# The second attention's step reordered, and its band's trip through memory in two halves

## The reference, cut to what matters

```python
q = _heads(x @ Wq)                      # x after a layernorm; 16 heads of 64
k = _heads(ctx_t @ Wk); v = _heads(ctx_t @ Wv)          # 77 text rows
sim = jnp.einsum('bihd,bjhd->bhij', q, k) * SCALE
dist = jnp.clip(jnp.arange(77)[None, :] - jnp.arange(nq)[:, None], -16, 16) + 16
sim = sim + jnp.einsum('bihd,ijd->bhij', q, rel_k[dist]) * SCALE
attn = jax.nn.softmax(sim, axis=-1)
out = jnp.einsum('bhij,bjhd->bihd', attn, v) + jnp.einsum('bhij,ijd->bihd', attn, rel_v[dist])
out = out + stream(Wk_ip, Wv_ip, ctx_i) * (jnp.tanh(alpha) + 1.0)
out = out + stream(Wk_ap, Wv_ap, ctx_a) * (jnp.tanh(beta) + 1.0)
return out.reshape(b, nq, 1024) @ Wo + bo               # added to x by the caller
```

## Time and profile before

| what | value |
|---|---|
| median of 3 runs | 1164.21 us (1162.24 to 1169.32) |
| profiled execution, its own time | 1165.82 us |
| its span | 1164.0 us |
| mean granted TensorE clock | 0.961 of full |
| PE, PEld, DVE, ACT, POOL busy | 1009.1, 792.3, 665.6, 406.5, 386.7 us |

### The profile page before, as it was taken

One profiled execution on the slowest core, in us unless ns is written; L12 is line 12 of the kernel. 1 busy time (PEld: TensorE's weight loads), 2 busy tenths in 40 slices (PEclk: granted clock), 3 DMA queues, 4 the chain that ended last, 5 costly groups with the idle time before them and its releaser, 6 DMA issues. The chain is left out here.

```text
span 1164.0 us, 23711 instructions
## 1 busy us (share of the span) xinstructions
PE 1009.1 (87%) x7428; PEld 792.3 (68%) x7429; DVE 665.6 (57%) x1607; ACT 406.5 (35%) x877; POOL 386.7 (33%) x481
## 2 busy tenths in 40 slices
PE   4888888845899999979997999999998985899996
PEld 4676666743466666647365888888887964888885
DVE  2788877764233333321105777677676572699994
ACT  2554444421222222213332445444453441222221
POOL 1243333431122222235001554644544432133332
PEclk9999999967999999989999999999999987899998
DMA  4444444334811111136673679888887752011110
GB/s 120 126 141 141 137 138 133 128 122 160 293 45 45 45 42 48 45 96 233 239 241 112 167 212 224 200 229 211 209 226 187 175 142 49 28 42 41 41 32 28
DMA packets 193657, 153.41 MB, mean 132 GB/s; under 512 B 130368, under 2 KB 176960, under 8 KB 193472
## 3 DMA queue, kind: packets, MB, share of 16 engines
q1 hardware_dynamic: 173568, 93.70, 30.6%
q10 hardware_dynamic: 16960, 50.58, 11.7%
q0 software_dynamic: 3072, 8.39, 2.3%
HBM read 84.80 MB, written 67.83 MB: 131 GB/s over the span
## 5 line engine op out<-in xcount | busy, mean ns | idle before, releaser
L1462 POOL TENSOR_TENSOR c_soft<-c_soft,c_share 128x616 f32<-128x616 f32 (+2 forms) x96 | 71.7, 774 | 136.5 <-DVE c_share L1890 134.6
L968 POOL TENSOR_TENSOR b_up<-b_up,b_gate 128x512 f32<-128x512 f32 x39 | 49.4, 1267 | 189.0 <-DVE b_up L1095 189.0
L2176 PE MATMUL d_CV<-d_hp,ffn_tap 128*128 128x128 f32 x768 | 95.3, 282 | 3.8 <-DVE d_hp L2253 3.4
L2176 PEld LDWEIGHTS d_CV<-d_hp,ffn_tap 128*128 128x128 f32 x768 | 90.9, 197 | 7.9 <-DVE d_hp L2253 5.1
L494 PE MATMUL a_M<-early 128*128 128x128 f32 x512 | 73.3, 289 | 9.3 <-ACT early L411 9.3
L1029 PE MATMUL b_G<-moe_w,b_rowsT 128*128 x156 | 76.0, 610 | 3.1 <-ACT b_rowsT L977 2.7
L1060 PEld LDWEIGHTS b_Y<-moe_w,b_hidT 128*128 128x128 f32 x312 | 59.3, 190 | 25.1 <-issue 19.2
L1060 PE MATMUL b_Y<-moe_w,b_hidT 128*128 x312 | 73.8, 380 | 0.8 <-ACT b_hidT L993 0.8
L494 PEld LDWEIGHTS a_M<-early 128*128 128x128 f32 x512 | 63.4, 196 | 16.0 <-ACT early L411 7.5
L1029 PE MATMUL b_U<-moe_w,b_rowsT 128*128 x156 | 73.4, 593 | 0.0
L1092 DVE TENSOR_TENSOR b_gate<-b_G,moe_b 128x512 f32<-128x512 f32 x39 | 27.0, 692 | 71.1 <-PE b_G L1029 70.3
(11 more groups left out here) (234 smaller groups left out, 2286.6 us busy)
## 6 DMA issues: line engine op xcount, KB each, us to landing
rel_windows<-c_relw ACTq DMA_DIRECT2D x32, 816.0 KB, 6.3
c_bias<-rel_windows SPq DMA_DIRECT2D x16, 616.0 KB, 4.9
prob_rows<-c_soft SPq DMA_DIRECT2D x16, 616.0 KB, 5.4
moe_w<-in_L_Wl SPq DMA_DIRECT2D x16, 512.0 KB, 3.8
values<-c_soft ACTq DMA_DIRECT2D x15, 512.0 KB, 3.4
b_rows<-expert_lists SPq DMA_DIRECT2D x39, 128.0 KB, 2.1
expert_out<-b_out SPq DMA_DIRECT2D x39, 128.0 KB, 1.7
c_v<-values SPq DMA_DIRECT2D x16, 308.0 KB
```

The lines of the kernel that those rows point to most:

```text
L968: nc.gpsimd.tensor_tensor(up[p][:, :], up[p][:, :], gate[p][:, :], ALU.mult).then_inc(g["hid"], 1)
L1462: ins = nc.gpsimd.tensor_tensor(soft[p][:, hs, a:z], soft[p][:, hs, a:z], share[:, s, hs].unsqueeze(2).to_broadcast([P, HS, z - a]), ALU.mult)
L2176: ins = nc.tensor.matmul(CV[:, m, :], tap[:, m, k, :], hp[p][:, m, k:k + P], start=(k == 0), stop=(k == 2))
```

## The change

- PE's step: `rows` of b+2 come right behind the first scores; `queries` are two calls of `query`; one ready piece (the first key tile in an odd step, the first half of the queries in an even one) stands between `weighted` 2 and 3 of b-1; `bands` and `output` of b-1 come last. ACT's order follows.
- DVE and POOL work on the rows of b+3 instead of b+2, DVE at its step's end, ahead of `output`; `ends` of b-1 moves behind the first `shares`. The rows of batch 2 are made in the setup.
- The residual plus bias is kept for all 16 batches (`x2b`, 16 KB a partition) and made by DVE in `rows`; POOL's `residual` is gone. For batches 0 to 2 the folded part of the bias is added in the setup by one DVE instruction of 768 columns.
- `prob_out` and `band_in` go by halves of 8 heads, each `prob_out` behind its own half's `normalise`. SP's order at the step's end is now: both `prob_out`, `rel_in` of b+2, both `band_in`, the store.
- The windows' zeros are written to memory once in the setup, by two DMAs out of a tile of 112 zeros; the window DMAs write rows of 92 numbers a head, no longer one run of 8 x 204.
- `far` has 61 columns a head, not 77 (`tails` and `ends`).
- In the setup DVE waits for the small weights before the first `rows`, and for the values' landing before the steps.

```diff
-        x2b = [sb(f"c_x2b{p}", [P, D]) for p in two]
+        x2b = sb("c_x2b", [P, NB, D])
...
-        relw = [sb(f"c_relw{h}", [P, HS, RELW]) for h in two]
+        relw = [sb(f"c_relw{h}", [P, HS, RELW - REL_LO - 1]) for h in two]
...
-            def prob_out(b, i, p):
-                apart(sp, g["soft"], 2 * b + 2)
-                since(sp, s_pin[p], 16 * i)
-                sp.dma_start(prob_d[p][:, :, MAXREL:MAXREL + TEXT], soft[p][:, :, 0:TEXT]).then_inc(s_pout[p], 16)
-
-            def band_in(b, i, p):
-                sp.wait_ge(s_pout[p], 16 * (i + 1))
-
-
-                sp.dma_start(band[p][:, :, 0:NSTEP - 1], sheared(prob_d[p], 1, 1, P, NSTEP - 1)).then_inc(s_pin[p], 16)
+            def prob_out(b, i, p, h):
+                hs = slice(h * HS, (h + 1) * HS)
+                apart(sp, g["soft"], 2 * b + h + 1)
+                since(sp, s_pin[p], 32 * i)
+                sp.dma_start(prob_d[p][:, hs, MAXREL:MAXREL + TEXT], soft[p][:, hs, 0:TEXT]).then_inc(s_pout[p][h], 16)
+
+            def band_in(b, i, p, h):
+                hs = slice(h * HS, (h + 1) * HS)
+                sp.wait_ge(s_pout[p][h], 16 * (i + 1))
+
+
+                sp.dma_start(band[p][:, hs, 0:NSTEP - 1], sheared(prob_d[p][:, hs, :], 1, 1, P, NSTEP - 1, HS)).then_inc(s_pin[p], 16)
...
-            sp.wait_ge(g["x2"], 1)
-            load(2, 0)
+            for p in two:
+                sp.wait_ge(g["x2"], p + 1)
+                load(2 + p, p)
+            sp.wait_ge(s_clear, 1)
+            for p in two:
+                sp.dma_start(rel_d[p][:, :, 0:REL_LO + 1], zeros[:, :].unsqueeze(1).to_broadcast([P, NH, REL_LO + 1])).then_inc(s_blank, 16)
...
+            sp.wait_ge(s_blank, 32)
...
+                    prob_out(b, i, p, h)
+                if there(b + 2):
+                    rel_in(b + 2, i + 1, p)
+                for h in two:
+                    band_in(b, i, p, h)
                 if not first:
                     store(b - 1, 1 - p)
-                band_in(b, i, p)
-                if there(b + 2):
-                    rel_in(b + 2, i + 1, p)
...
-                nc.gpsimd.tensor_tensor(far[:, :, :], soft[p][:, :, 0:TEXT],
-                                        cst("behind_band").unsqueeze(1).to_broadcast([P, NH, TEXT]), ALU.mult).then_inc(g["tails"], 1)
+                nc.gpsimd.tensor_tensor(far[:, :, :], soft[p][:, :, MAXREL:TEXT],
+                                        cst("behind_band")[:, MAXREL:TEXT].unsqueeze(1).to_broadcast([P, NH, TEXT - MAXREL]), ALU.mult).then_inc(g["tails"], 1)
...
-            residual(0, 0)
 
             def steps(b, i, p, first, last):
-                if there(b + 2):
-                    inverse_std(b + 2, p)
-                if there(b + 3):
-                    gather(b + 3, 1 - p)
+                if there(b + 4):
+                    gather(b + 4, p)
                 for h in range(2):
                     normalise(b, p, h)
+                if there(b + 3):
+                    inverse_std(b + 3, 1 - p)
                 tails(b, p)
-                if there(b + 1):
...
             def windows(b, i, p):
 
-                lo, hi = REL_LO + 1, REL_LO + NREL
+                hi, end = NSTEP, RELW - REL_LO - 1
                 for h in two:
                     n, k = turns.next()
                     act.wait_ge(g["filled"], n + 1)
                     since(act, s_relout[h], 16 * b)
                     r, w = T[k][:, 0:HS * NSTEP].rearrange("p (h r) -> p h r", h=HS), relw[h]
-                    nc.scalar.activation(w[:, :, lo:hi], r, ACT.Copy)
-                    nc.scalar.activation(w[:, :, hi:RELW], r[:, :, NSTEP - 1:NSTEP].to_broadcast([P, HS, RELW - hi]), ACT.Copy)\
+                    nc.scalar.activation(w[:, :, 0:hi], r, ACT.Copy)
+                    nc.scalar.activation(w[:, :, hi:end], r[:, :, NSTEP - 1:NSTEP].to_broadcast([P, HS, end - hi]), ACT.Copy)\
                         .then_inc(g["emptied"], 1)
                     act.wait_ge(g["emptied"], n + 1)
                     since(act, s_relin[p], 16 * i)
-                    act.dma_start(rel_d[p][:, h * HS:(h + 1) * HS, :], w[:, :, :]).then_inc(s_relout[h], 16)
+                    act.dma_start(rel_d[p][:, h * HS:(h + 1) * HS, REL_LO + 1:RELW], w[:, :, :]).then_inc(s_relout[h], 16)
 
             def exps(b, p, h):
...
-                    behind(b - 1)
-                if p == 1 and there(b + 2):
-                    projected(kT, PAIR_TILES[:2])
-                    exps(b, p, 0)
-                    projected(kT, PAIR_TILES[2:])
-                    exps(b, p, 1)
+                    for k in range(4):
+                        probs(k)
+                exps(b, p, 0)
+                if p == 1 and ahead:
+                    projected(kT, PAIR_TILES[:1])
+                if not first:
+                    attended(b - 1, 0)
+                if p == 1 and ahead:
+                    projected(kT, PAIR_TILES[1:2])
+                if p == 0 and ahead:
+                    query(p, 0)
+                exps(b, p, 1)
+                if p == 1 and ahead:
+                    projected(kT, PAIR_TILES[2:3])
+                if not first:
+                    attended(b - 1, 1)
+                if p == 1 and ahead:
+                    projected(kT, PAIR_TILES[3:])
+                    query(p, 0)
+                if ahead:
+                    query(p, 1)
+                    windows(b + 2, i + 1, p)
                 if not first:
                     bands()
-                if there(b + 2):
-                    rows()
-                if p == 0 or not there(b + 2):
-                    for h in two:
-                        exps(b, p, h)
-                if there(b + 2):
-                    queries(p)
-                    windows(b + 2, i + 1, p)
 
             by_batch(steps)(act)
...
+                between[0]()
                 pe.wait_ge(s_vin[p], 16 * NS * (i + 1))
-                for k in range(4):
-                    weighted(b, p, k, n[k])
-                    if k < 2:
-                        n.append(probabilities(b, p, k + 2))
+                weighted(b, p, 0, n[0])
+                n.append(probabilities(b, p, 2))
+                weighted(b, p, 1, n[1])
+                n.append(probabilities(b, p, 3))
+                weighted(b, p, 2, n[2])
+                between[1]()
+                weighted(b, p, 3, n[3])
+
+            def nothing():
+                pass
 
             def steps(b, i, p, first, last):
                 turns.begin(b, i, p)
+                ahead = there(b + 2)
                 scores(b, i, p, 0)
+                if ahead:
+                    n_rows = rows(b + 2, p)
+
+                def second_scores():
+                    scores(b, i, p, 1)
+
+                def ready_work():
+                    if p == 1 and ahead:
+                        context(i + 1)
+                        projected(wk[0], PAIR_TILES[:1])
+                    elif ahead:
+                        query(n_rows, 0)
+
+                if first:
+                    second_scores()
+                    ready_work()
+                else:
+                    attend(b - 1, i - 1 + p, 1 - p, [second_scores, ready_work])
+                if p == 1 and ahead:
+                    projected(wk[0], PAIR_TILES[1:])
+                    query(n_rows, 0)
+                if ahead:
+                    query(n_rows, 1)
+                    distances(p)
                 if not first:
-                    n_probs = [probabilities(b - 1, 1 - p, 0), probabilities(b - 1, 1 - p, 1)]
-                scores(b, i, p, 1)
-                if not first:
-                    attend(b - 1, i - 1 + p, 1 - p, n_probs)
-                if p == 1 and there(b + 2):
-                    context(i + 1)
-                    projected(wk[0])
-                if not first:
-                    n_bands = bands(b - 1, i - 1 + p, 1 - p)
-                if there(b + 2):
-                    n_rows = rows(b + 2, p)
-                if not first:
-                    output(b - 1, n_bands)
-                if there(b + 2):
-                    queries(n_rows)
-                    distances(p)
...
+                nc.vector.tensor_tensor(biased_rows(b), x2[p][:, :], bo[:, :], ALU.add).then_inc(g["x2b"], 1)
...
             nc.vector.tensor_copy(first_v[:, :], relT["v"][:, 0:1].to_broadcast([P, P])).then_inc(s_steps, 1)
 
+            dve.wait_ge(g["filled"], FIRST_ROWS + 1)
...
+            folded = S[:, HS:HS + KD, :].rearrange("p k n -> p (k n)")
+            dve.wait_ge(g["x2b"], 3)
+            nc.vector.tensor_tensor(x2b[:, 0:3, :], folded.unsqueeze(1).to_broadcast([P, 3, D]), x2b[:, 0:3, :], ALU.add).then_inc(s_folded, 1)
+            nc.vector.tensor_tensor(bo[:, :], folded, bo[:, :], ALU.add).then_inc(s_folded, 1)
...
             def steps(b, i, p, first, last):
-                if there(b + 3):
-                    pick_rows(b + 3, i + 1 + p, 1 - p)
-                if there(b + 2):
```

(16 more changed lines are left out.)

114 lines of the change are left out of this document (62 added, 52 removed).

## The result

The changed kernel took 1170.59 us (median of 20 runs, 1167.41 to 1172.72), the kernel before beside it 1164.32 us (20 runs). The ratio is 1.0042, 95% interval 1.0029 to 1.0054 (the quotient of the two medians is 1.0054; the text goes by the ratio): slower by 0.4%, inside the 1% called no change, and 17.6 us above the forecast of 1153, outside its range.

The account below looks back on a forecast made before the run. PE's own stream was taken to set the step. Setup +1.5, steps 0 and 1 -1.0, plain and special steps -5.2 and the end -6.5 summed to -11.2 us, giving 1153 us from the 1164.21 median; range 1145 to 1162.

Parts of the forecast that it names:

- DVE in the plain step: Even plain step: DVE's work stays hidden, next rows ready at 17.7 us, PE asking at 20.0; 1.2 and 2.3 us in hand.
- a new wait, most likely for DVE's rows: Sign of a wrong forecast: an odd step over 23.6 us would mean PE waits anew, for DVE's rows or the band.
- The end: Step 14 to the end: halves and earlier `less_max` of step 15 bring 50.9 us to 44; sum -6.5 us, bounds -4 and -9.
- Setup: Before the attention: an added DVE instruction (0.5 us) and two DMAs of zeros (1.0 us) cost +1.5 us.
- Steps 0 and 1: First two steps: the 3.69 us wait goes, PE waits over 4 us for batch 3's rows; 39.5 us for 40.5, -1.0.
- Special steps: Steps 2 and 12: their band waits get cover, losing 1.1 and 4.4 us against 19.2 us, together -5.5 us.
- Plain steps of PE: PE in plain steps: band wait of 0.85 us goes, added costs come; even 18.9 us, odd 23.1, pair unchanged at 42.0.
- the fills: Costs on PE from the new order of work in plain steps: 0.57 us per even step, 0.25 net per odd one.
- Full DMA engines: Rival, chance 0.06: the windows' 368-byte packets take 54 ns, not 27, fill the DMA engines and cost 28 us; 1181 us.
- a further doubling for writes: Window DMAs: by the skill's rule, writes to memory in rows of 368 bytes could cost twice their share.
- Free fills: Rival, chance 0.16: PE's queue hides the 0.57 us per step in 12 steps, 6.8 us less; 1146 us.
- Waits that only move: Rival, chance 0.22: gaps of steps 12 (4.4 us) and 2 (1.1) stay, step 1 may cost 3 more; 1161 us.

Follow-up runs that it names:

- a_hold: The changed kernel, but POOL starts `tails` of batch b only when DVE has written batch b+3's normalised rows; ratio 0.9985 to the kernel before.
- b_ends: The changed kernel, but in steps 14 and 15 `ends` of the batch before stands ahead of the two row maxima; ratio 0.9985 to the kernel before.
- m_abd: The changed kernel with `tails` held for the rows, `ends` first in steps 14 and 15, batch 3's rows in the setup; zeros kept; 1157.82 us, ratio 0.9921.
- n_allagain: The kernel of e_all measured again, on the same chip as m_abd; 1152.94 us, ratio 0.9879 to the kernel before.
- f_halves: The kernel before with one edit: the probabilities' trip out and the band's trip back in two halves of 8 heads; 1152.15 us, ratio 0.9868.
- e_all: The changed kernel with `tails` held for the rows, `ends` first in steps 14 and 15, whole windows without zeros, batch 3's rows in setup; 1153.03 us, ratio 0.9869.
- h_again: The changed kernel itself measured again, on another call's chip; ratio 1.0043 to the kernel before.

## Why the prediction was wrong, point by point

**DVE in the plain step: the step that failed most.** I wrote that `rows_normal` ends 17.7 us after the first scores and PE asks at 20.0, "1.2 us in hand at the one place and 2.3 at the other". PE did ask at 20.0 in step 6 (786.0 less 765.98); the rows were there at 20.8. The failed step is the term for DVE's own time at the end of the step. Two durations in it were short, both taken from rows in which POOL held nothing up: the additions of the gathered rows (2.42 us for the two in place of 0.97, which makes the start of `rows_normal` 18.5 and not 17.3), and `rows_normal` itself (2.37 in place of 0.41), since the reordered step puts `tails` on POOL right behind the 1/std that releases DVE. The 2.3 us of slack are spent, and 0.94 more, in five odd steps: 4.9 us in steps 2 to 13 (a_hold). Steps 0 and 1 took 40.72 us in a_hold, 41.71 and 42.86 in the two traces of the changed kernel, so 1.0 to 2.1 us more. With the second term taken away 1.1 us of slack are left, so the first costs nothing by itself. I had named "a new wait, most likely for DVE's rows" as what an odd step over 23.6 would show; it did. What I hadn't done is to ask for each instruction on DVE what POOL runs at that moment; the 2.88 us of the kernel before's step 1 were there to be found.

**The end.** Forecast 44 us, measured 49.7 (44 is 6.9 under the 50.9 of the earlier trace rows; my sum took 6.5, a slip of 0.4). I placed `ends` between the shares of step 15 and counted it for DVE only; but PE's band transposes wait for it, and in steps 14 and 15 nothing else is left for PE. Two waits of 4.33 us, of which b_ends brings back 3.5 us in all, since the band (2.40 us) and ACT (3.87 us) are next. So 3.5 of the 5.8 us over the forecast are shown to be this term. The rest stands against those two waits, of which the forecast had only 1.0 us for a band; how it splits between them isn't shown.

**Setup.** Forecast +1.5, with 0 to 3 us for the zeros, and I took 1.0. They cost 3.8 by the means of 18 traces and 4.9 by the medians of m_abd and n_allagain, above my upper bound: I summed the DMA engines' time for them, 8.4 us of all engines, and not who is queued beside them. The 5.6 us of the first trace split otherwise: 1.2 were there before the attention, in code that wasn't changed; 1.7 are PE's wait for the short context, 8.88 us in this trace and 7.0 to 7.3 in the 17 others; 2.2 are the zeros; and 0.64 is the added DVE instruction, for which I had taken 0.5. So the mechanism was named and its size was wrong, and over half of that row's miss is chance.

**Steps 0 and 1.** The mechanism was right (PE waits over 4 us for batch 3), its size not: rows at 18.4 us after the first scores, not 16.4, 2.0 of them the lock. The wait of 2.38 us for `c_qT`, which ACT copies behind the exponentials, was missed.

**Special steps.** The waits of steps 2 and 12 went: 18.86 and 18.90 us against 20.26 and 23.57. That is -6.1 us, against -5.5 forecast (which was counted to 19.2, the plain step of before). In the odd steps it was given back: 143.3 us for the six, 137.2 before.

**Plain steps of PE.** 18.86 us against 18.9, and 23.07 against 23.1 with the lock taken away. With no waits in the old order (f_halves) they are 18.41 and 22.87, so the fills cost 0.45 and 0.20 us, forecast 0.57 and 0.25.

**The rivals.** Full DMA engines (1181): refuted. q10's share fell to 15.1% from 18.5%, and the windows land in 5.4 us, not 6.4. Its 29120 packets, nearly all of 368 bytes, took 15.1% of 16 engines over 340 us: 28 ns each, where I had worked out 27, so the rival's 54 ns are refuted. Per byte they are dearer, as I had written: 13 bytes per ns of an engine, against 23 for the long runs of before (250 ns for 5.8 KB on average). The rule of 512 bytes for line rate in the Trainium skill (DMA: Bandwidth & Descriptors, Specifications) agrees with that; a further doubling for writes doesn't show. Free fills: refuted by the 0.45. Waits that only move was the nearest case in kind, though not by the gaps that it named.

**What no case held.** That the halves and the order take away the same waits. I gave the halves a worth only in steps 14 and 15. Alone they took 15.1 and 15.6 us off the kernel before (medians on the two chips), in the new order nothing. And that the mended kernel, e_all, ends at the 1153 us of the forecast is luck: its steps 0 and 1 are 3 us under the forecast's, its end 2 us over.

## What to carry to other kernels

When one change holds two cures for the same wait, price each of them alone: here the small one (a transfer cut in two, so that its way back starts while its way out is under way) gave 1.3%, and the large one spent as much in new waits as it saved. Before an instruction is moved on VectorE, look at what GpSimd runs in the new place, because here a cover of 2 us was gone with one neighbour. And where steps at the end of a pipeline have no later work, they need an order of their own.

## What the runs showed of the hardware

- A VectorE instruction of 0.41 us (SBUF to SBUF, 256 columns, f32) took 2.36 us when it started within 0.05 us of a GpSimd TENSOR_TENSOR of 2.27 us, and 1.32 us when that was cut in two. GpSimd wasn't slowed: its instruction took 2.26 to 2.28 us in all 16 batches, also in the last three, where no `rows_normal` stood beside it.
- Not every VectorE instruction is held. Beside the same GpSimd work an SBUF-to-SBUF copy of 2 columns took 1.78 us in place of 0.15, but an addition that reads PSUM kept its 0.42 us (both a_hold), and reductions from SBUF to SBUF kept their 1.33 and 1.17 us beside `normalise` (776.6 to 779.1 us of the changed kernel).
- Two DMAs of 896 KB in runs of 448 bytes took 11.5 to 12.9 us to land (median, in the four traces after, b_ends, h_again and m_abd) and held transfers of another queue up: the short keys landed in a median of 3.7 to 4.3 us there, 2.0 to 2.9 in five traces without them, and single waits for them were up to 4.57 us (b_ends).
- Writes of 368 bytes took 28 ns of an engine each, 13 bytes per ns, and runs of 5.8 KB on average 250 ns, 23 bytes per ns; 816 KB in large runs and 368 KB in small ones land in about the same time, 6.4 and 5.4 us.
